# Four plain gathers of GpSimd under way in place of two, with a short iota behind each request

## The reference

```python
def _fff(x, nw, nb, w1, b1, w2, b2, act):
    node = jnp.zeros(x.shape[:2], dtype=jnp.int32)
    for _ in range(DEPTH):
        logit = jnp.einsum('bsd,bsd->bs', x, nw[node]) + nb[node]
        node = 2 * node + 1 + (logit > 0).astype(jnp.int32)
    leaf = node - NN
    h = act(jnp.einsum('bsd,bsdl->bsl', x, w1[leaf]) + b1[leaf])
    return jnp.einsum('bsl,bsld->bsd', h, w2[leaf]) + b2[leaf]

q = _fff(xn, ...q..., relu); k = _fff(xn, ...k..., relu); v = _fff(xn, ...v..., relu)
att = softmax(q k^T / sqrt(D)); y = xn + att v
return y + _fff(y, ...f..., gelu)
```

## Time and profile before

| | us |
|---|---|
| median of 3 runs | 1434.96 (1433.56 to 1436.65) |
| the profiled execution's own time | 1447.87 |
| its span, from the first to the last instruction | 1446.1 |
| TensorE busy | 1201.3 (83% of the span) |
| VectorE busy | 888.7 (61%) |
| ScalarE busy | 581.1 (40%) |
| GpSimd busy | 447.2 (31%) |
| mean granted TensorE clock | 0.938 of full speed |

### The profile page before, as it was taken

How to read it: one execution, slowest core, us unless ns; L and a number is a source line. 1 busy time by engine, 2 the same in 40 slices (tenths; PEclk the granted TensorE clock), 3 DMA queues, 4 the chain that set the end, 5 groups by cost and what they waited for, 6 DMA issues and landing times. The chain is left out here.

```text
span 1446.1 us, 24458 instructions
## 1 busy us (share of the span) xinstructions
PE 1201.3 (83%) x7104; PEld 874.9 (61%) x7108; DVE 888.7 (61%) x2537; ACT 581.1 (40%) x1106; POOL 447.2 (31%) x593
## 2 busy tenths in 40 slices
PE   1398899999886887799596757958999889999997
PEld 1295677777765666577465645635666555555554
DVE  7998989999722575647273454745666625353534
ACT  2125566555422225467362314615666531212110
POOL 2248344454455035443432406441211000000000
PEclk9999999999897998899797987968999999999999
DMA  9000000000001732658336614560100000000000
GB/s 278 7 2 2 1 1 1 1 1 1 0 1 23 234 108 77 214 196 286 124 109 190 190 37 88 120 156 8 16 9 9 2 1 1 15 0 15 0 15 15
DMA packets 92612, 92.23 MB, mean 64 GB/s; under 512 B 27080, under 2 KB 77770, under 8 KB 92492
## 3 DMA queue, kind: packets, MB, share of 16 engines
q1 hardware_dynamic: 80204, 65.59, 14.6%
q0 software_dynamic: 12288, 25.18, 7.1%
HBM read 76.05 MB, written 14.68 MB: 63 GB/s over the span
## 5 line engine op out<-in xcount | busy, mean ns | idle before, releaser
L3427 ACT ACTIVATE m_silu<-m_psG 128x512 f32<-128x512 f32 x48 | 28.7, 598 | 213.5 <-PE m_psU L3547 213.5
L3480 DVE TENSOR_TENSOR m_act<-m_silu,m_psU 128x512 f32<-128x512 f32 x48 | 33.0, 688 | 120.9 <-ACT m_silu L3427 105.6
L2192 PE MATMUL gq_psH<-gq_xT,gq_w 128*128 (+1 forms) x564 | 100.6, 304 | 6.5 <-issue 3.5
L2192 PEld LDWEIGHTS gq_psH<-gq_xT,gq_w 128*128 128x128 f32 x564 | 80.4, 203 | 33.1 <-issue 29.0
L2202 PE MATMUL gq_psY<-leaf_w,gq_hT 128*128 (+1 forms) x282 | 90.8, 405 | 6.7 <-DVE gq_hT L2078 6.2
L2078 DVE SCALAR_TENSOR_TENSOR gq_hT<-gq_xT,unit_leaf,gq_act 128x128 f32<-128x128 f32 x141 | 49.6, 352 | 70.0 <-ACT gq_act L1910 40.4
L3547 PE MATMUL m_psG<-m_xnT,m_gate 128*128 128x512 f32 x192 | 90.7, 594 | 2.1 <-PEq L192 2.1
L3547 PE MATMUL m_psU<-m_xnT,m_up 128*128 128x512 f32 x192 | 90.2, 592 | 0.0
L1796 POOL DMA_INDIRECT gq_x<-rows_x,gq_token_i x48 | 47.1, 982 | 101.5 <-DVE gq_tile_row L2071 53.9
L765 DVE MATCH_REPLACE8 s_product_a_rest<-a_top,s_product_a_rest 128x256 f32<-128x256 f32 x192 | 76.1, 412 | 0.3 <-issue 0.3
L2960 DVE TENSOR_REDUCE c_max<-c_psA 128x4 f32<-128x1024 f32 x32 | 39.2, 1225 | 56.9 <-PE c_psA L3108 56.9
(11 more groups left out here) (561 smaller groups left out, 3054.5 us busy)
## 6 DMA issues: line engine op xcount, KB each, us to landing
leaf_w<-in_group_w SPq DMA_DIRECT2D x128, 128.0 KB
leaf_w<-in_group_w SPq DMA_DIRECT2D x64, 256.0 KB
a_w<-in_L_xattn_W SPq DMA_DIRECT2D x2, 1024.0 KB, 12.9
rows_x<-token_rows SPq DMA_DIRECT2D x8, 256.0 KB, 4.9
sorted_y_q<-gq_y SPq DMA_DIRECT2D x16, 128.0 KB, 5.9
sorted_y_k<-rows_ahead SPq DMA_DIRECT2D x16, 128.0 KB, 4.9
sorted_y_v<-gq_y SPq DMA_DIRECT2D x16, 128.0 KB, 2.5
rows_f<-token_rows SPq DMA_DIRECT2D x8, 256.0 KB
```

What stands on the lines that cost most here:

```text
L2192: last = pe.matmul(psH[n % 2][:, 0:P], w1[n % 3][:, c, :], xT[:, c, bass.ds(g * -P + u * P, P)], start=(c == 0), stop=(c == DC - 1))
```

## The change

The limit of two requests under way becomes four (`UNDER_WAY`) in `gather`, `seed` and `fetch`. In `RowsAhead.pool` a group of two gathers (q or k of one batch) now waits for the group two before it, in place of the one before it. A new class `Rests` puts one `iota` (64 whole numbers in one partition, into a buffer that nobody reads) behind each of these requests; before each such iota GpSimd waits for the iota before it. The gathers that add, and the iota that makes `column_i`, stay as they are.

```diff
--- before.py
+++ after.py
@@ -1652,6 +1652,25 @@
         self.weights.load(sp)
 
 
+UNDER_WAY = 4
+
+
+class Rests:
+
+
+    def __init__(self, core, ctx, name):
+        self.line = core.sb(ctx, name + "_rest", [1, 64], I32)
+        self.over = core.sem(name + "_rested")
+        self.n = 0
+
+    def __call__(self, pool):
+        if self.n:
+            pool.wait_ge(self.over, self.n)
+        self.n += 1
+        pool.iota(self.line[:], pattern=[[1, 64]], base=0, channel_multiplier=0
+                  ).then_inc(self.over, 1)
+
+
 class RowsAhead:
 
 
@@ -1664,19 +1683,18 @@
         self.landed = [[core.lasting_sem(f"rows_ahead_{w}{b}") for w in "qk"]
                        for b in range(self.BATCHES)]
 
-    def pool(self, pool):
+    def pool(self, pool, rest):
         for b in range(self.BATCHES):
             for n in range(2):
-                if n:
-                    pool.wait_ge(self.landed[b][0], 16 * ST)
-                elif b:
-                    pool.wait_ge(self.landed[b - 1][1], 16 * ST)
+                if b:
+                    pool.wait_ge(self.landed[b - 1][n], 16 * ST)
                 for t in range(ST):
                     pool.indirect_dma_start(
                         self.rows[:, b, n, t, :], None, self.core.sorted_y[n],
                         bass.IndirectOffsetOnAxis(
                             self.core.back[:, n, b * ST + t:b * ST + t + 1], 0)
                         ).then_inc(self.landed[b][n], 16)
+                    rest(pool)
 
 
 def group_products(core, name, first, nf, leaves, weights, places, rows, beside, gelu=False,
@@ -1781,7 +1799,7 @@
         with nc.Block() as block:
             @block.gpsimd
             def _(pool):
-                under_way = []
+                under_way, rest = [], Rests(core, own, name)
 
                 def gather(f, t):
 
@@ -1790,13 +1808,14 @@
                         pool.wait_ge(found_in, f + 1)
                     if n >= RING:
                         pool.wait_ge(x_ps, n - RING + 1)
-                    if len(under_way) >= 2:
-                        pool.wait_ge(*under_way[-2])
+                    if len(under_way) >= UNDER_WAY:
+                        pool.wait_ge(*under_way[-UNDER_WAY])
                     under_way.append((tile_in[n % RING], 16 * (n // RING + 1)))
                     pool.indirect_dma_start(
                         xs[n % RING][:], None, core.rows_x if route else core.rows_f,
                         bass.IndirectOffsetOnAxis(token_i[:, f, t:t + 1], 0)
                         ).then_inc(tile_in[n % RING], 16)
+                    rest(pool)
 
                 def seed(f, t):
 
@@ -1831,7 +1851,7 @@
                     for n in range(2):
                         for t in range(NT):
                             pool.wait_ge(stored[n][t], 16)
-                    ahead.pool(pool)
+                    ahead.pool(pool, rest)
                 else:
                     pool.wait_ge(core.rows_out, 16 * B)
                     for t in range(NT):
@@ -2387,13 +2407,13 @@
 
             @block.gpsimd
             def _(pool):
-                under_way = []
+                under_way, rest = [], Rests(core, own, "t")
 
                 def fetch(b, n):
 
                     for t in range(ST):
-                        if len(under_way) >= 2:
-                            pool.wait_ge(*under_way[-2])
+                        if len(under_way) >= UNDER_WAY:
+                            pool.wait_ge(*under_way[-UNDER_WAY])
                         here = rows_in[b % SLOTS4][n][t]
                         pool.indirect_dma_start(
                             rows_of(b, n)(t), None, core.sorted_y[n],
```

## The result

The changed kernel took 1390.99 us (median of 4 runs, 1388.38 to 1392.69) where the kernel before took 1435.81 in the same comparison: a ratio of 0.9683, 95% interval 0.9658 to 0.9708. The profiled execution is 1392.69 us, with a span of 1391.0.

A forecast was written before the change was run, and what follows sets the result against it. GpSimd's limit of two gathers under way, which keeps TensorE waiting, was taken as the bound. 22.0 (q, k, v) + 11.9 (attention) + 0 (f) = 33.9 us, taken as 29 off the 1434.96 median: 1406 us, range 1397 to 1424.

The forecast's parts named there:

- the excess of the profiled run: Profiled execution lay 12.9 us above the runs' median; gain on the median between 33.6 and 21.0 us, 29 taken.
- The time lost behind the waits: TensorE at its lower clock after waits: 2.2 us behind v's tile 11, 2.1 and 1.4 us in attention.
- The signs that the prediction gave for being right: Among them: TensorE's gq_x waits under 3 us, v's seeds over before 680, 1.3 to 1.6 us apart, attention's four waits gone.
- The pace, p = 1.5 us: Mean time per GpSimd request with four under way, the larger of issue (1.4 us) and landing (1.2 us at most).
- the lower bound: The iota behind each gather costs from nothing, inside the 0.30 us gap, to 0.40 us; 0.15 taken.
- Functions q, k, v: 22.0 us: TensorE's 19.8 us of waits for gathered tiles go, plus 2.2 us at lower clock after v's tile 11.
- Over before TensorE: The 16 fetches ahead for attention, behind v's tile 15, take 24 us from about 692, ending before TensorE.
- Token attention: 11.9 us: Waits of 9.9 us go, plus 2.1 and 1.4 us of low clock, less 1.5 us for meeting weight loads.
- Function f: 0: Its 16 gathers already take 1.54 us each, the new pace: zero gain, between -0.5 and +0.5.
- A: Rival, 22%: attention gains nothing because weight loads keep their DMA share; only q, k, v's 22.0 us go, 1415 us.
- B: Rival, 9%: gathers are served one after another, so the wait for a landing only moves; 1435 us.
- C: Rival, 9%: plain gathers issue slower with more under way, 2.24 us a request; 16 us more, 1451 us.

The follow-up runs named there:

- the first comparison: The changed kernel against the kernel before, chip not on record: 1390.99 against 1435.81 us, ratio 0.9683.
- chip 8: Four partial changes against the kernel before: pieces alone 1.0009; the limit of four only in q, k, v 0.9766, only in attention 0.9919, only in f 0.9998.
- chips 0 and 14: The unaltered change against the kernel before: 1516.1 us, ratio 1.0488, on chip 0; 1509.37 us, ratio 1.0495, on chip 14.
- the version with two or three pieces: The change with more iotas behind each request, against the kernel before: three 0.9863 (chip 12), 0.9864 (chip 14); two 0.9861 (chip 14), 0.9882 (chip 7).

## Why the prediction was right and wrong

The size is where it went wrong, in three terms of the sum. TensorE's wait at the end of the fetches ahead, worth 6.1 us, was left out. 4.9 us were taken off for the excess of the profiled run, most of which lay elsewhere. The time lost behind the waits was set 5.8 us too small.

*What bounds the kernel, and the direction.* Right for the first comparison: all waits of the earlier trace rows for gathered tiles are gone, v's tile 11 follows at once, and no load of weights took their place. The signs that the prediction gave for being right are all there: v's 16 seeds are over at 665.87, 1.55 us apart in the mean, the longest wait of such a request for a gather's landing is 2.1 us, and a piece takes 0.17. That the direction came out right also needed a comparison in which TensorE's results are not held, and nothing in the prediction asked for that. That part was luck.

*The pace, p = 1.5 us.* It is 1.29. The piece costs 0.04 us over the 1.25 without it, near the lower bound; I had 0.15. Landings hold GpSimd back for 10.7 us over all the requests. Nothing hangs on this, as by the prediction's own sums every wait goes for any p up to 1.6.

*Functions q, k, v: 22.0 us.* 27.8 in the pair of profiles. The waits themselves are the 19.8 that I had. What is short is the time behind them, 8.0 us in place of 2.2: from v's tile 11 to the end of v it took 44.2 us before and 40.5 after, 3.7 less (granted clock 0.60 for the first 7 us before, 1.00 after). From q's first turn to v's it took 132.9 and 125.5, 7.4 less, of which the waits are 3.6. The other 0.6 lie between v's first tile and tile 11. The mechanism held, the size was 5.8 short. The waits also differ from run to run: with the old order, chip 8 shows 20.6, 24.0 and 25.1 us for `gq_x`, 17.3 to 17.9 of them before tile 11 in place of 16.2.

*The step that was missing: the end of the fetches ahead.* "Over before TensorE" was said of them, and no term came of it. Before the change the last of them ended at 757.05, just after TensorE's last unit at 756.95, and the way into attention went by GpSimd; the 11.18 us of `POOLq` before its first request were the hint. It is worth 6.1 us, which the limit in q, k and v alone collects as well (10.9 to 4.7 us).

*Token attention: 11.9 us.* 13.3 in the profiles, 11.6 by the experiment. *Function f: 0.* 0, by the experiment.

*The excess of the profiled run.* I took 29 of 33.9, since the 12.9 us above the median might lie in the stalls. At least 7.6 us of them lay elsewhere, in f, where the limit is worth nothing. This step cost 33.9 - 29 = 4.9 us, nearly as much as the missing one. With it left out, the missing term put in and the two sizes corrected, the sum is 27.8 + 6.1 + 13.3 = 47.2, against 44.8.

*The rivals.* A and B have fallen by the limit in attention alone: 11.6 us where both had nothing. C foresaw "slower with more under way" from gathers that themselves get slower, and they didn't. Yet on chips 0 and 14 the sign is C's, by a way that I had nowhere: the gathers keep their 0.95 us and the other engines pay. No row of the profile before could give its size; GpSimd there had no row of more than four plain gathers without a wait. I asked what a faster GpSimd would collide with and looked only at the DMA.

The Trainium skill ("SBUF — State Buffer", "Who interferes with whom") says of engines in SBUF that "only the shared port pair causes contention", the pair that VectorE and GpSimd share, and by it GpSimd could be made to wait by VectorE. The traces show no such wait of weight: the gathers of the change take 0.95 us at the median in all three comparisons, single ones up to 1.9. What they do show has no place in that rule. TensorE's results came up to 18 us late, for ScalarE and for VectorE. Whether that is contention for a port at all is open.

## What to carry to other kernels

A limit on requests under way can be a spacing in disguise: before raising it, ask what the engine's longest unbroken row will be and what else runs beside it. Then space the requests as widely as the consumers allow. Here TensorE waited 1.4 us in all for gathered tiles with a request every 1.53 us, and 18.0 with one every 1.77. Time a change and each variant of it in one comparison, and a change that turns on DMA issue on more than one chip, before its sign is believed: the version with two or three pieces, 1.2 to 1.4% faster on chips 12, 14 and 7, is the safer one, though the change as it stands was 3.2% faster on the first.

## What the runs showed of the hardware that was not expected

- Comparisons differ in kind and not by a fraction: one kernel was 0.968 of the kernel before in one and 1.049 and 1.050 in two others, while the kernel before moved only between 1435.8 and 1444.3 us. That the chip makes the difference was not shown.
- On chips 0 and 14 a row of indirect gathers, one every 1.25 to 1.29 us, keeps TensorE's results from ScalarE and VectorE, for 12 and 18 us at the longest places read on chip 0, and lets them go 3.4 to 4.2 us after the row's last gather is issued; at 1.53 us TensorE is still idle a quarter of the stretch, at 1.77 us not at all. The cause in the chip is open, and why one comparison has it and another not.
- An iota of 64 numbers on one partition, put between two gathers that follow each other directly, costs 0.04 us of GpSimd's time: it fills a gap that is there anyway.
- From GpSimd's last fetch before a change of stage to its first after it pass 11.2 us where it comes last, in five profiles alike (11.18 to 11.21); TensorE's own share of the change is 4.6 to 4.7.
